# An in-projection in scaled fp16 parts, with twelve staging places for its weights

## What is computed

```python
u  = x @ in_proj_w.T + in_proj_b                  # 3*512 columns, per sequence
uc = short_conv(u, short_w) + short_b             # 3 taps, causal
x0, x1, v = split(uc)
k  = sine_network(positions) * decay              # one filter, made once
y  = (fftconv(v * x1, k) + filter_bias * ...) * x0
x  = layernorm(x + y @ out_proj_w.T + out_proj_b)
x  = layernorm(x + down((silu(gate(x))) * up(x))) # 1408 hidden, integer codes
```

## Time and profile before

| | us |
|---|---|
| median of three runs | 994.12 (993.87 to 994.49) |
| the profiled execution | 995.0 |
| its span in the profile | 993.2 |

### The profile page before, as it was taken

One profiled execution on the slowest core, in us unless ns is written; L12 is line 12 of the kernel. 1 busy time (PEld: TensorE's weight loads), 2 busy tenths in 40 slices (PEclk: granted clock), 3 DMA queues, 4 the chain that ended last, 5 costly groups with the idle time before them and its releaser, 6 DMA issues.

```text
span 993.2 us, 17112 instructions
## 1 busy us (share of the span) xinstructions
PE 961.9 (97%) x6099; PEld 761.5 (77%) x6188; DVE 721.9 (73%) x1345; ACT 426.7 (43%) x929; POOL 571.7 (58%) x628
## 2 busy tenths in 40 slices
PE   6999999999999999999999999999999999999996
PEld 5577777878777777778777887777787777777774
DVE  5498876968777687767868677876877677685454
ACT  3676534433353434434443343443334344333342
POOL 3689773755647476464747646465664746575210
PEclk8999999999999999999999999999999999999998
DMA  7655201121122101221102211111111110001100
GB/s 235 206 170 133 49 1 19 26 64 23 43 43 63 20 5 43 44 64 22 44 5 39 64 22 44 32 47 31 21 43 22 44 22 22 23 3 42 43 22 22
DMA packets 98952, 47.96 MB, mean 48 GB/s; under 512 B 80048, under 2 KB 84784, under 8 KB 98868
## 3 DMA queue, kind: packets, MB, share of 16 engines
q1 hardware_dynamic: 98370, 46.79, 18.1%
q10 hardware_dynamic: 498, 0.08, 0.0%
HBM read 32.17 MB, written 8.39 MB: 41 GB/s over the span
## 4 chain that ended last, share of the span: by engine, by line
PE 87%; issue 4%; DVE 3%; POOL 3%; ACT 1%; DMA 1%; SPq 0%; POOLq 0%; DVEq 0%
PE gate_up L1135 14%; PE gate_up L1136 14%; PE bank L995 11%; PE bank L997 11%; PE bank L996 11%; PE down L1148 8%; PE down L1147 5%; PE bank L1095 5%; PE spectrum L995 1%; PE spectrum L996 1%; PE spectrum L997 1%; PE bank L1070 1%; POOL acc L766 1%; DVE tmp L906 1%; DMA x<-in_win 1%
## 5 line engine op out<-in xcount | busy, mean ns | idle before, releaser
L765 POOL TENSOR_TENSOR acc<-acc,tmp 128x256 f32<-128x256 f32 x160 | 123.3, 771 | 150.3 <-DVE tmp L906 138.6
L729 ACT ACTIVATE hid<-gate_up,gate_scale 128x256 f32<-128x256 f32 x176 | 82.7, 470 | 212.5 <-PE gate_up L1136 212.4
L906 DVE TENSOR_TENSOR tmp<-spectrum,filt 128x512 f32<-128x512 f32 x256 | 172.7, 680 | 0.4 <-PE spectrum L997 0.4
L1135 PE MATMUL gate_up<-x2T_hi,wg_sb 128*128 128x256 f16 x704 | 163.4, 273 | 0.0
L1136 PE MATMUL gate_up<-x2T_lo,wg_sb 128*128 128x256 f16 x704 | 163.3, 273 | 0.0
L1135 PE MATMUL gate_up<-x2T_hi,wu_sb 128*128 128x256 f16 x704 | 163.3, 273 | 0.0
L1136 PE MATMUL gate_up<-x2T_lo,wu_sb 128*128 128x256 f16 x704 | 163.3, 273 | 0.0
L759 POOL TENSOR_TENSOR acc<-acc,tmp 128x512 f32<-128x512 f32 x96 | 127.7, 1331 | 61.3 <-DVE tmp L906 60.8
L995 PE MATMUL bank<-xT_hi,win_hi 128*128 128x512 f32 x360 | 149.5, 415 | 2.8 <-POOL win_lo L747 2.5
L997 PE MATMUL bank<-xT_hi,win_lo 128*128 128x512 f32 x360 | 143.5, 399 | 0.0
L996 PE MATMUL bank<-xT_lo,win_hi 128*128 128x512 f32 x360 | 143.0, 397 | 0.0
(11 more groups left out here) (170 smaller groups left out, 1826.8 us busy)
## 6 DMA issues: line engine op xcount, KB each, us to landing
x<-in_x SPq DMA_DIRECT2D x28, 256.0 KB, 2.8
out<-x SPq DMA_DIRECT2D x28, 256.0 KB, 2.1
xstage<-in_x SPq DMA_DIRECT2D x96, 64.0 KB, 2.6
xstage<-in_x SPq DMA_DIRECT2D x12, 256.0 KB, 4.2
x<-in_win SPq DMA_DIRECT2D x12, 256.0 KB, 6.0
acc<-in_decay SPq DMA_DIRECT2D x4, 256.0 KB
x<-in_wout SPq DMA_DIRECT2D x4, 256.0 KB, 2.8
x2T_hi<-in_wu SPq DMA_DIRECT2D x4, 256.0 KB, 3.8
```

Of the source, the lines that this page charges most:

```text
L765: G.tensor_tensor(acc[:, i, 0, :], acc[:, i, 0, :], t[:, 1, :], ALU.subtract)
L906: TT(dst, spectrum[j % 2][:, :, :], k_part, ALU.mult).then_inc(made_done, 1)
L1135: mm(dst, w[:, kb, rows(q)], x2T_hi[:, kb, ts], start=kb == 0, stop=False)
```

## The change

- The in-projection's parts of weights and x become fp16. Before the split, each is multiplied by a power of two, so that its greatest value fits the format. For x there is one scale per sequence; for the weights one for each of six groups of two tiles (`GROUP_OF_FLOAT`). The inverse scales are folded into the taps of the short convolution.
- A scale is made so: `xmax`/`wmax`, DVE's greatest absolute value along each row (one `tensor_reduce` per tile of 128x512); `xs`/`ws`, a matmul with a matrix of ones that sums these over partitions; `xscale`/`wscale`, four small dependent DVE instructions; `wtaps`, two more for the taps.
- Weight low parts of the in-projection move from POOL to DVE, as does the wait of the PE for them (`w_lo_done`).
- There are twelve staging places, so weight tiles 4 to 11 are issued by SP right behind the taps, ahead of the network's last matrix, the decay and the codes.
- The sum for x of a later sequence takes a turn in the ring of banks: in beat 6 (beat 8 for sequence 1), behind that beat's products.

```diff
+STAGES = 12
+GROUP_OF_FLOAT = {0: 0, 1: 0, 2: 1, 3: 1, 4: 2, 5: 2, 7: 3, 8: 3, 9: 4, 10: 4, 11: 5, 12: 5}
+    if n % 2 == 1 and n + 1 < HALVES and beat == (6 if (n + 1) // 2 in BY_SQUARES else 8):
+        steps += [("xs", (n + 1) // 2)]
...
-            steps += [("xturn", following, beat - 2)]
+            steps += [("xmax", following, beat - 2), ("xturn", following, beat - 2)]
+    if n == 1 and beat == 6:
+        steps += [("xmax", 1, tb) for tb in range(TB)]
...
+SCALED_IN_BEAT = {0: (1, 2), 1: (3,), 2: (4,), 4: (5,)}
+def group_steps(g):
+    return [("wmax", k) for k in GROUP_OF_FLOAT if GROUP_OF_FLOAT[k] == g] + [("ws", g), ("wscale", g), ("wtaps", g)]
...
     if n == 0:
+        for g in SCALED_IN_BEAT.get(beat, ()):
+            steps += group_steps(g)
         steps += {1: [("sin", 0), ("net", 1), ("arg", 1)], 2: [("sin", 1), ("arg", 2)], 3: [("net", 2), ("sin", 2)],
                   4: [("kmm", d) for d in range(TB)]}.get(beat, [])
...
-    steps = [("xt", 0, 0), ("xt", 0, 1), ("xsplit", 0, 0), ("xsplit", 0, 1), ("stage", 0), ("stage", 1), ("xt", 0, 2),
-             ("xt", 0, 3), ("xsplit", 0, 2), ("xsplit", 0, 3), ("net", 0), ("arg", 0), ("bias", ), ("scales", )]
+    steps = [(kind, 0, tb) for tb in range(TB) for kind in ("xt", "xmax")] + [("xs", 0), ("xscale", 0)]
+    steps += [("wmax", 0), ("wmax", 1), ("ws", 0), ("wscale", 0), ("stage", 0), ("stage", 1)]
+    steps += [("xsplit", 0, tb) for tb in range(TB)] + [("wtaps", 0), ("net", 0), ("arg", 0), ("bias", ), ("scales", )]
...
-        win_hi, win_lo = (sb(f"win_{n}", [P, CB, 3 * D], F32R) for n in ("hi", "lo"))
+        win_hi, win_lo = (sb(f"win_{n}", [P, CB, 3 * D], F16) for n in ("hi", "lo"))
...
-        xT_hi, xT_lo = (sb(f"xT_{n}", [P, CB, L], F32R) for n in ("hi", "lo"))
+        xT_hi, xT_lo = (sb(f"xT_{n}", [P, CB, L], F16) for n in ("hi", "lo"))
...
+            for k in range(4, STAGES):
+                load_float(k)
             for k in range(2):
                 sp.dma_start(out_bias[half_of(k), :], w3).then_inc(w3_in, 16)
...
+                elif kind == "wscale":
+                    g, = at
+                    least, scale = w_inv[:, g:g + 1], w_scale[:, g:g + 1]
+                    dve.wait_ge(sums_done, g + 2)
+                    Vv.tensor_reduce(least, first_sums[:, 8 * g + 8:8 * g + 11], axis=mybir.AxisListType.X, op=ALU.add)\
+                        .then_inc(sums_read, 1)
+                    dve.wait_ge(sums_read, g + 2)
+                    TS(least.bitcast(I32), least.bitcast(I32), EXPONENT, None, ALU.bitwise_and).then_inc(w_step, 1)
+                    dve.wait_ge(w_step, 3 * g + 1)
+                    TS(least, least, INTO_RANGE, None, ALU.mult).then_inc(w_step, 1)
+                    dve.wait_ge(w_step, 3 * g + 2)
+                    Vv.reciprocal(scale, least).then_inc(w_scaled, 1)
+                elif kind == "stage" and at[0] in GROUP_OF_FLOAT:
+                    k, = at
+                    g = GROUP_OF_FLOAT[k]
+                    dve.wait_ge(stage_hi, k + 1)
+                    STT(out=floats[k][2], in0=float_slot(k), scalar=w_scale[:, g:g + 1], in1=floats[k][1],
+                        op0=ALU.mult, op1=ALU.subtract).then_inc(w_lo_done, 1)
...
                     if n < 2:
-                        pe.wait_ge(stage_used, (0, 7)[n] + 2 * t + 2)
+                        pe.wait_ge(w_lo_done, 2 * (3 * n + t) + 2)
...
+                elif kind == "xs":
+                    s, = at
+                    dst, done = (first_sums, sums_done) if s == 0 else (free_bank(use["xs", s]), bank_ready)
+                    pe.wait_ge(x_max, TB * (s + 1))
+                    mm(dst[:, :TB + 1], ones[:, :], x_stat[:, s % 2, :], start=True, stop=True).then_inc(done, 1)
+                elif kind == "ws":
+                    g, = at
+                    pe.wait_ge(w_max, 2 * g + 2)
+                    mm(first_sums[:, 8 * g + 8:8 * g + 11], ones[:, :], w_stat[:, g, :], start=True, stop=True)\
+                        .then_inc(sums_done, 1)
```

129 lines of the change are left out of this document (102 added, 27 removed).

## The result

The changed kernel takes 1030.14 us (median of 4 runs, 1029.15 to 1031.98), the kernel before beside it 994.18: ratio 1.0364, 95% interval 1.0346 to 1.0382. It is slower by 36 us. The forecast was 1018 with a range to 1028: the sign and most steps of the mechanism were right, the size was 12 us short and the range 2 us. The profiled execution spans 1028.0 us.

A forecast was written before the change was run, and what follows sets the result against it. TensorE bounds the long middle; at the start the engines' step order counts, with VectorE and GpSimd nearly full from 60 to 80 us. 995.0 + 27.5 + 4.2 + 10.1 - 17.6 = 1019.2, less 0.9: 1018, range 1004 to 1028.

The forecast's parts named there:

- The gain: Projection matmuls in fp16: pace 0.2155 to 0.2157 instead of 0.233 us, 84 of 96 products counted, 17.6 us saved.
- Prices on VectorE: Added start instructions: maximum 0.60 us, low part 0.65, group of weights 2.9; 25 us added to VectorE's queue.
- The trip: In each scale, VectorE to one tiny TensorE matmul and back: 0.45 us, between 0.3 and 0.9.
- The order of the queue: On TensorE at the start, `ws 3` precedes the first product, which starts at 31.8 us instead of 12.93.
- The start: From first loads to v's transposes, which start at 66.0 us instead of 38.47: cost 27.5 us, between 21 and 34.
- The third product waits behind `ws 4`: In the start on TensorE: the third projection product runs from 44.4 to 47.0 us, after the maxima of tiles 9 and 10.
- a clock that falls in the two idle gaps: TensorE's clock in the start's gaps of some 4 us: counted only inside the upper end of 34.
- The tiles ahead: Eight weight tiles loaded earlier in the start: SyncE's waits go, decay, matrix and codes still in time; nothing either way.
- Sequence 1: Four maxima (2.4 us) and scale with taps (1.0) in VectorE's full stretch delay the last low part: 4.2, between 2 and 6.
- The ring: From n=3, x's sum takes a bank turn in beat 6 of odd halves: 7.0 plus 3.1, 10.1 us, between 5 and 12.
- The n=3 stall: In the ring at n=3, the inverse `iv (2, 2)` waits for the conv ending at 152.40 instead of starting at 149.37: 3.1 us.
- the start is longer: Rival: VectorE's instructions slowed, trips of 0.9, clock fallen in the gaps; start 38, sum 1029; 13%.

The follow-up runs named there:

- e4: The unscaled kernel: the kernel before with fp16 in place of float32r for both parts of x and weights, no scaling; 978.55 us, ratio 0.9823.
- e5: Changed kernel plus 17 and 22 unused matmuls on TensorE ahead of the weight sums of groups 4 and 5; 1028.40 us, ratio 1.0333.
- e1: Changed kernel with the first projection product placed behind group 2's taps instead of behind `sin 0`; 1026.70 us, ratio 1.0314.
- e11: e4 plus the twelve staging places and the eight weight tiles loaded early, still no scaling; 984.18 us, ratio 0.9885.
- e13: e10 with weight tiles 4 to 11 loaded behind the codes again; 991.02 us, ratio 0.9950.
- e6: Changed kernel with weight tiles 4 to 11 loaded behind the codes again, twelve staging places kept; 1030.11 us, ratio 1.0350.
- e9: Changed kernel with sequence 0's scale of x used for all sequences, without x's later maxima, sums and scales; 1016.55 us, ratio 1.0219.
- e8: Changed kernel with sequence 1's maxima moved to beats 9 and 10 of n=0 and its sum to beat 2; 1033.47 us, ratio 1.0381.
- e3: Changed kernel with x's sums from sequence 2 on written to spare columns of an inverse's bank, outside the ring; 1027.71 us, ratio 1.0311.
- e14: e10 with x's parts in the plain forms: copy without scale on ScalarE, plain subtraction on VectorE; 993.75 us, ratio 0.9987.
- e10: Changed kernel with all scales the constant 1 and no maxima, sums or scales, rest of the change kept; 997.34 us, ratio 1.0021.
- e7: Changed kernel with weights' scales the constant 1, without their maxima, sums and scale steps, x's scales kept; 1010.13 us, ratio 1.0145.
- e12: Changed kernel with weights' scales the constant 1 and sequence 0's scale of x for all sequences; 998.37 us, ratio 1.0028.
- e15: e12 with tiles 4 to 11 loaded behind the codes again and the weights' low parts on GpSimd; 990.76 us, ratio 0.9954.

## Why the prediction fell short, step by step

It forecast 1018 and named the start as the term with the most room. Its steps:

- **The gain, 17.6.** Right: 17.6 by e4, pace 0.215.
- **Prices on VectorE.** Right to a few per cent: 2.99 for a group (2.9), 1.27 for two maxima, 0.66 for a low part (0.65). The trip was mis-sized, 0.68 idle (0.45), and that too is the clock: 0.48 in e5.
- **The order of the queue.** Right: `ws 3` ahead of the first product, 33.12 (31.8). e1 shows that the product's place was worth 2.5 us by the traces and 5 by the ratio.
- **The start, 27.5.** Measured 33.4, inside its bounds of 21 to 34. The step that failed: "The third product waits behind `ws 4`: 44.4 to 47.0", with "a clock that falls in the two idle gaps of some 4 us is inside the upper end". It had seen the gaps and left the clock out of the likeliest value. Up to the maxima of tiles 9 and 10, which end at 44.28 (forecast 44.2), VectorE is on time. Then the third product goes from 44.78 to 49.85, 5.07 us, where e5 needs 2.58. The filter's four multiplications are 0.86 apart, in e5 0.43, and VectorE waits for them. Five matmuls of the sixth product also go at 0.43, and the transform starts right behind it, 1.0 after VectorE has the filter ready (67.56). At v's transposes e5 puts the clock at 4.9 of the 5.9 that were missing. The other 1.0 is a low part held beside GpSimd: tiles 9 and 10 take 2.33 (55.66 to 57.99) where 1.3 was forecast, while GpSimd multiplies from 55.89 to 57.52, and e5 has the same 2.35. Only some 3 of the clock's term reach gu 0.
- **The tiles ahead, "nothing either way".** Wrong as a rule and nearly right as a sum: e11 shows 6.2 us and e13 7.1 where nothing covers them; in this kernel 1.25 us of wait, and 1.4 of time by e6's ratio, not told from nothing. It asked what was late behind the tiles, looked at decay, matrix and codes, and missed the two small loads of scales at 18 us.
- **Sequence 1, 4.2.** v's transposes are at +33.4 and gu 0 at +38.3, so 4.9, inside 2 to 6; e9, without it, goes from +32.6 to +31.3, so by that account 6.2, just outside. The parts that the forecast names add to 3.4 (2.4 and 1.0), and the other 0.8 has no source in it. Its place is a wait of 3.1 in front of the sum. e8 shows that the place can't be chosen freely.
- **The ring, 10.1.** The n=3 stall was the forecast one, 2.80 (3.1); the stretch from gu 0 to gu 12 costs 4.8 by e9. In the odd halves 5 to 13 the step is there as forecast, five times 1.42 (1.4), though most of it is the sum's own wait for `ln1` and its two small matmuls and not a wait of `op`. The loss from gu 16 to 126 is 8.4 (12.64 - 4.26): these 7.1 and 1.3 in small steps. What the forecast lacked is what lies under the stall. Without the sum in the ring only 2.9 come back (e3), and with no sum at all 3.3 (e9), as then the scaled forms of x's parts cost 4.9 (e14 against e10). It had priced these forms, instructions that keep their number and grow in length, at nothing. In this kernel nothing of that size is left beside the stall (of the 1.3, e14 with the plain forms has 0.9 too), so the 7.0 came out right. What leaving the sum out would give is well under it.

**The sum of the misses.** In the spans the change is 34.8 us (1028.0 - 993.2), and the forecast's terms add to 24.2. By the ledger the measured terms are: start 33.4, sequence 1 4.9, the stretch to gu 16 4.8, the odd halves 8.4, less 15.9 that the unscaled kernel gains from v's transposes to the end (16.39 - 0.53), less 0.7 at the tail, where the changed kernel falls 1.33 behind gu 126 and the unscaled one 0.68. So the 10.6 between are, by 0.1, start 5.9, sequence 1 0.7, the stretch to gu 16 1.7, the odd halves 1.4, the gain that came short 1.7, less the tail's 0.7. The other 1.2 of the twelve: the profiled execution of before lay 0.9 above its median, this one (1029.82) 0.3 below. The rival "the start is longer" had the right mechanism, with 13%, down to a slowed instruction of VectorE. Its time of 1029 rested on a start of 38, more than was there, so that it came within 1 us is luck.

**What eats the gain, by experiment.** From e4 (0.9823) to the changed kernel (1.0364) are 53.8 us: weights' maxima and groups 21.8 (e7), x's later scales 11.6 (e12 against e7), x's first scale 0.7 (e12 against e10), tiles ahead 7.1 (e13 against e10), scaled forms of x's parts 3.4 (e14 against e10). The remaining 9.2 belong to the weights' low parts on VectorE, the order of the start and the taps. They weren't separated. e15 differs from e13 in two things, the low parts on GpSimd and x's first scale, and their ratios are 0.04% apart with intervals that overlap. The traces say where to look: v's first transposes are at 43.63 in e13 and at 43.97 in e15, but at 37.94 in e4. The plain forms would take 1.4 of this (50.21 in e14, 51.58 in e10). So some 4 of the 9 lie in the start, and they are there with the low parts on either engine. Terms are as measured in that order, the last two both from e10, with no run that has both; e9 gave 14.4 for x's later scales when the weights' were still there, and of the 21.8 some 1 to 2 hang on the use of the ratio, as said above.

**Open.** Why the clock falls behind the gap of 2.15 us in some executions and not in others; where e5's 4.9 at v's transposes shrink to 3.0 at gu 0; and whether an instruction of VectorE and one of GpSimd really wait for each other, which was read from the traces and not tested.

## What to carry to other kernels

A data path that is 17 us faster can be eaten by the steps that it needs: here the start alone grew by 33 us, behind dependent steps on VectorE. Count the statistics, their trips and each instruction that only gets longer, and try the path without them first. A step that waits for a load holds everything behind it in its engine's queue, so ask of every load issued earlier which small load now comes later and who stands behind its reader. A gap on TensorE costs its own length and, where the clock falls, the slower matmuls behind it; both belong in the likeliest value, not only in the upper bound.

## What the runs showed of the hardware

After 3.91 us without work TensorE's matmuls of 512 columns went at 0.43 us, the 1.2 GHz level, for 5.07 us and more, then at 0.22. After 5.08 us it was the same for some 6 us. With the first gap filled to 0.24 they stayed at 0.22. After a gap of 2.15 us in a full stretch the clock fell in 6 of 17 traces. A row maximum over 128x512 costs VectorE 0.58 to 0.60 in a row (0.67 alone). The trip from VectorE over one tiny matmul and back leaves it idle 0.68 with TensorE at its lower level, 0.48 with the gap before it filled by matmuls. A ScalarE copy of 128x512 is 0.706 with a scale operand and 0.614 without. VectorE's scaled low part is 0.75, at times 1.30, against 0.67 to 0.69 for the plain subtraction. Where it takes 1.30 beside GpSimd's 128x256 sum, that takes 0.72, and where it takes 0.73, GpSimd's takes 1.30.
